# A six-layer decoder on one core: the routing of both expert mixtures rewritten, and the softmax behind the second routing moved down VectorE's queue

## The reference, cut to what matters

```python
def _L0_ffn_ref(hidden_states, Wr, W1, b1, Wo, bo, gamma, beta):
    router_logits = x @ Wr.T
    expert_idx = jnp.argmax(jax.nn.softmax(router_logits, axis=-1), axis=-1)
    for e in range(E):
        mask = (expert_idx == e)[:, None].astype(x.dtype)
        inter = inter + mask * jax.nn.gelu(x @ W1[e] + b1[e], approximate=False)
...
def _L1_ffn_ref(x, Wr, br, W1, b1, W2, b2):
    cap = max(1, int(T / E * CAPACITY_FACTOR))            # 40 slots of each of 8 experts
    probs = jax.nn.softmax(x @ Wr + br, axis=-1)
    topk_p, topk_e = jax.lax.top_k(probs, K)              # K = 2
    oh = jax.nn.one_hot(e_flat, E, dtype=jnp.int32)
    pos_all = jnp.cumsum(oh, axis=1) - oh                 # place of a token in its expert's slots
    keep = pos < cap
    h = jax.nn.relu(jnp.einsum('enc,ech->enh', buf, W1) + b1[:, None, :])
    y = jnp.einsum('enh,ehc->enc', h, W2) + b2[:, None, :]
    y_tok = y_tok * (p_flat * keep.astype(x.dtype))[:, :, None]
```

## Time and profile before

| | |
|---|---|
| median of 3 runs | 1101.97 us (1101.78 to 1103.04) |
| the profiled execution's own time | 1103.46 us |
| its span in the profile | 1101.5 us |
| PE busy | 1053.6 us, 96% of the span |
| DVE busy | 724.1 us, 66% |
| ACT busy | 643.1 us, 58% |
| POOL busy | 167.1 us, 15% |

### The profile page before, as it was taken

The page is one execution under the profiler, slowest core; times in us unless marked ns, Lnnn a source line. Parts: engine busy times, 40 slices in busy tenths (PEclk is TensorE's granted clock), DMA queues, the critical chain, the costliest instruction groups (busy, mean ns, idle before and its releaser), DMA issues.

```text
span 1101.5 us, 23000 instructions
## 1 busy us (share of the span) xinstructions
PE 1053.6 (96%) x9039; PEld 666.0 (60%) x9039; DVE 724.1 (66%) x1841; ACT 643.1 (58%) x1428; POOL 167.1 (15%) x237
## 2 busy tenths in 40 slices
PE   7999999998999999999899999999999999999987
PEld 5663665556875556555687366555578646655567
DVE  6641767889653386888955158688975417677871
ACT  5550557776763266777566136777666505587724
POOL 3320400121020130111112022021212004000000
PEclk9999999999999999999999999999999999999999
DMA  8400000000000000000000000000000000000000
GB/s 254 140 1 1 1 2 11 14 9 1 1 11 1 1 1 2 11 21 1 2 2 10 1 1 2 11 1 21 2 1 10 1 1 1 2 1 1 2 2 10
DMA packets 21083, 15.74 MB, mean 14 GB/s; under 512 B 887, under 2 KB 18660, under 8 KB 20972
## 3 DMA queue, kind: packets, MB, share of 16 engines
q1 hardware_dynamic: 20948, 14.24, 4.3%
q10 hardware_dynamic: 24, 0.01, 0.0%
HBM read 13.18 MB, written 1.05 MB: 13 GB/s over the span
## 4 chain that ended last, share of the span: by engine, by line
PE 72%; DVE 11%; ACT 9%; issue 5%; DVEq 2%; POOL 1%; POOLq 0%; ACTq 0%; DMA 0%
PE ps L786 11%; PE ps L1020 8%; PE ps L984 8%; PE ps L1002 5%; PE ps L828 3%; PE ps L822 3%; PE ps L1172 3%; PE ps L1163 3%; PE ps L1029 2%; ACT arena L1476 2%; PE ps L819 2%; PE ps L920 2%; DVE nmax L2186 2%; ACT arena L1239 2%; PE ps L880 2%
## 5 line engine op out<-in xcount | busy, mean ns | idle before, releaser
L1239 ACT ACTIVATE arena<-ps 128x512 f32<-128x512 f32 (+7 forms) x296 | 159.6, 572 | 111.3 <-PE ps L1002 55.6
L2186 DVE TENSOR_REDUCE nmax<-ps 128x1 f32<-128x512 f32 x256 | 164.4, 684 | 23.6 <-PE ps L984 22.9
L1476 ACT ACTIVATE arena<-ps,nmax 128x512 f32<-128x512 f32 x256 | 173.8, 685 | 7.9 <-DVE nmax L2186 4.8
L1652 POOL TENSOR_TENSOR rstd<-mv,neg_half 128x2 f32<-128x2 f32 x72 | 49.9, 695 | 660.6 <-DVE mv L1826 660.5
L1002 PEld LDWEIGHTS ps<-ident,arena 64*128 64x128 f32 x2048 | 76.5, 138 | 79.0 <-issue 45.4
L2191 DVE COPY arena<-ps 128x512 f32<-128x512 f32 x128 | 88.2, 689 | 47.5 <-PE ps L1002 47.2
L786 PE MATMUL ps<-big,w1a 128*128 128x512 f32 x256 | 117.3, 604 | 0.1
L1002 PE MATMUL ps<-ident,arena 64*128 64x64 f32 x2048 | 92.6, 228 | 8.1 <-ACT arena L1239 2.7
L2078 DVE TENSOR_TENSOR big<-XT,ps 128x512 f32<-128x512 f32 x32 | 22.0, 688 | 90.7 <-PE ps L771 90.4
L786 PEld LDWEIGHTS ps<-big,w1a 128*128 128x128 f32 x256 | 46.3, 189 | 57.7 <-issue 56.5
L1401 ACT ACTIVATE big<-ps 128x512 f32<-128x512 f32 x16 | 9.6, 597 | 116.4 <-PE ps L786 116.4
(11 more groups left out here) (393 smaller groups left out, 2009.1 us busy)
## 6 DMA issues: line engine op xcount, KB each, us to landing
ctx<-in_ctx_dram SPq DMA_DIRECT2D x4, 512.0 KB, 4.0
w1a<-in_L_ffn_W_dram SPq DMA_DIRECT2D x1, 2048.0 KB, 9.5
w1b<-in_L_ffn_W_dram SPq DMA_DIRECT2D x1, 2048.0 KB, 11.6
w2b<-in_L_ffn_W_dram SPq DMA_DIRECT2D x8, 256.0 KB, 6.0
X<-in_x_dram SPq DMA_DIRECT2D x4, 256.0 KB, 2.8
out_dram<-Y SPq DMA_DIRECT2D x3, 256.0 KB, 2.3
arena<-in_L_xattn_Wq_dram SPq DMA_DIRECT2D x1, 512.0 KB
arena<-in_L_xattn_Wk_dram SPq DMA_DIRECT2D x1, 512.0 KB
```

The costliest lines, as they stand in the source:

```text
L1239: return act.activation(dst, src, ACT.Copy)
L1476: act.activation(cprob[:, 2 * (t % 2) + h, :], bank(2 * (t % 2) + h), ACT.Exp, bias=nmax[:, s:s + 1], accum_out=rsum[:, j % 2, s:s + 1]).t ...
L2186: dve.tensor_reduce(nmax[:, s:s + 1], bank(s % 4), AX.X, ALU.max, negate=True)\
```

## The change

Three things change, in all four passes.

1. One-expert mixture: the four comparisons that make `onehot` become one instruction over all tiles. PE turns the one-hot before the keys (2, 0) instead of behind them, issues both picks one behind the other, and then the keys (3, 0), which go into bank 1 instead of bank 4. ACT copies `ohT` before the keys (2, 0).
2. Two-expert mixture, routing: the eight comparisons become two, the subtraction for the softmax goes behind the cast, the first half of the dispatch matrix is announced by itself (`disp_ready` counts two for each pass), and PE gathers the first sequence's tokens as soon as that half is there. The transposes that filled PE's time become fewer, and keys and values of the next pass are spread over the gaps. On ACT the exponentials come before the recurrence's sigmoid.
3. Two-expert mixture, softmax: sum, inverse and product of the exponentials go from between the cast and the places to the head of `combined()`, behind the recurrence's inverses, and a drain is added.

```diff
@@ PE, mixture_top1
                 project_v(0, 6, 1)
-                project_k(2, 7, 0)
                 keys_read(it, 0, 1)
                 pe.wait_ge(onehot_ready, it + 1)
...
                 last.then_inc(ohT_ps, 1)
+                project_k(2, 7, 0)
...
-                project_k(3, 4, 0)
                 pe.wait_ge(ohT_ready, it + 1)
                 pick_rows(0)
-                keys_read(it, 3, 0)
                 pick_rows(1)
+                project_k(3, 1, 0)
+                keys_read(it, 2, 0)
@@ PE, mixture_top2
                     turn_ctx(it + 1, 5)
-                    keep_awake(4, 4)
-                    for seq in range(GROUP):
-                        pe.wait_ge(ctxT_ready, (it + 1) * 2 + seq + 1)
-                        project_k(5, 3 + seq, seq)
+                    pe.wait_ge(ctxT_ready, (it + 1) * 2 + 1)
+                    project_k(5, 3, 0)
                 else:
-                    keep_awake(6, 32)
+                    keep_awake(6, 22)
...
-                    for seq in range(GROUP):
-                        project_v(5, seq, seq)
-                    keys_read(it + 1, 5, 1)
+                    pe.wait_ge(ctxT_ready, (it + 1) * 2 + 2)
+                    project_k(5, 4, 1)
+                    project_v(5, 0, 0)
                 else:
-                    keep_awake(6, 18)
-                pe.wait_ge(disp_ready, it + 1)
+                    keep_awake(6, 12)
                 for b in range(GROUP):
+                    if more:
+                        keys_read(it + 1, 5, b)
+                    pe.wait_ge(disp_ready, it * GROUP + b + 1)
...
+                if more:
+                    project_v(5, 1, 1)
                 pe.wait_ge(xb_ready, it * GROUP + GROUP)
...
-                    values_read(it + 1, 5, 1)
+                    values_read(it + 1, 5, 0)
                 up(0)
                 for e in range(E):
+                    if more and e == 0:
+                        values_read(it + 1, 5, 1)
@@ ACT, mixture_top2
                 if more:
-                    rec_receptance(it + 1, 7)
                     ctx_turned(it + 1, 5)
+                    keys(it + 1, 5, 3, 0)
                 act.wait_ge(e1_arg, it + 1)
                 act.activation(ex1[:, :, :], ex1[:, :, :], ACT.Exp).then_inc(e1_exp, 1)
                 if more:
-                    for seq in range(GROUP):
-                        keys(it + 1, 5, 3 + seq, seq)
-                    for seq in range(GROUP):
-                        context_values(it + 1, 5, seq, seq)
+                    rec_receptance(it + 1, 7)
+                    keys(it + 1, 5, 4, 1)
+                    context_values(it + 1, 5, 0, 0)
@@ DVE, mixture_top1
-                for t in range(TT):
-                    last = dve.tensor_scalar(onehot[:, t, :], iota_e[:, :], topf[:, t, 0:1], None, ALU.is_equal)
-                last.then_inc(onehot_ready, 1)
+                dve.tensor_tensor(onehot[:, :, :], iota_e[:, :].unsqueeze(1).to_broadcast([P, TT, PARTS * E]),
+                                  topf[:, :, 0:1].to_broadcast([P, TT, PARTS * E]), ALU.is_equal).then_inc(onehot_ready, 1)
@@ DVE, mixture_top2
-                for t in range(TT):
-                    dve.tensor_scalar(A[:, t, :], iota_e[:, 0:E], topf[:, t, 0:1], None, ALU.is_equal)
-                    dve.tensor_scalar(onehot[:, t, 0:E], iota_e[:, 0:E], topf[:, t, 1:2], None, ALU.is_equal)
+                for part, which in ((A[:, :, :], 0), (onehot[:, :, 0:E], 1)):
+                    dve.tensor_tensor(part, iota_e[:, 0:E].unsqueeze(1).to_broadcast([P, TT, E]),
+                                      topf[:, :, which:which + 1].to_broadcast([P, TT, E]), ALU.is_equal)
...
-                dve.wait_ge(e1_exp, it + 1)
-                dve.tensor_reduce(esum[:, :], ex1[:, :, :], AX.X, ALU.add)
...
+                for seq in range(GROUP):
+                    for t in tiles_of(seq):
+                        last = dve.tensor_tensor(slots(disp, t), iota_c[:, :].unsqueeze(1).to_broadcast([P, E, CAP]),
+                                                 per_expert(posA, t), ALU.is_equal)
+                    last.then_inc(disp_ready, 1)
                 dve.drain()
 
                 def combined():
+                    dve.wait_ge(e1_exp, it + 1)
+                    dve.tensor_reduce(esum[:, :], ex1[:, :, :], AX.X, ALU.add)
+                    dve.drain()
+                    dve.reciprocal(einv[:, :], esum[:, :])
```

More of the change, by code:

```diff
@@ L1540, in mixture_top2 @@
                     copy(xb[:, b, :], ps[:, 3 + b, 0:SLOTS]).then_inc(xb_ready, 1)
+                if more:
+                    context_values(it + 1, 5, 1, 1)
                 W = GROUP * CAP
@@ L2299, in mixture_top2 @@
                 dve.drain()
-                dve.tensor_tensor(ex1[:, :, :], lg[:, :, :], top[:, :, 0:1].to_broadcast([P, TT, E]), ALU.subtract)\
-                    .then_inc(e1_arg, 1)
                 for t in range(TT):
@@ L2313, in mixture_top2 @@
                 dve.tensor_copy(A_bf[:, :, :], A[:, :, :]).then_inc(two_hot, 1)
[L2315 to L2320 removed]
+                dve.tensor_tensor(ex1[:, :, :], lg[:, :, :], top[:, :, 0:1].to_broadcast([P, TT, E]), ALU.subtract)\
+                    .then_inc(e1_arg, 1)
                 dve.wait_ge(pos_ps, it + 1)
@@ L2331, in per_expert @@
                     return m[:, t, :].unsqueeze(2).to_broadcast([P, E, CAP])
-                for t in range(TT):
-                    last = dve.tensor_tensor(slots(disp, t), iota_c[:, :].unsqueeze(1).to_broadcast([P, E, CAP]),
-                                             per_expert(posA, t), ALU.is_equal)
-                last.then_inc(disp_ready, 1)
+                for seq in range(GROUP):
[3 more added lines that the diff above has]
+                    last.then_inc(disp_ready, 1)
                 dve.drain()
                 def combined():
+                    dve.wait_ge(e1_exp, it + 1)
+                    dve.tensor_reduce(esum[:, :], ex1[:, :, :], AX.X, ALU.add)
+                    dve.drain()
+                    dve.reciprocal(einv[:, :], esum[:, :])
+                    dve.drain()
+                    dve.tensor_tensor(ex1[:, :, :], ex1[:, :, :], einv[:, :].unsqueeze(2).to_broadcast([P, TT, E]),
+                                      ALU.mult)
+                    dve.drain()
                     for t in range(TT):
```

10 lines of the change are left out of this document (3 added, 7 removed).

## The result

The changed kernel takes 1094.87 us (median of 4 runs, 1094.07 to 1095.72); the kernel before took 1101.88 (4 runs, 1101.74 to 1103.04). The ratio is 0.993, with a 95% interval of 0.9915 to 0.9945. The prediction was 1094.9.

The account below looks back on a forecast made before the run. The prediction took PE's pace as the bound (72% of the last chain), with DVE's queue nearly tied. Its terms, 4 × 0.5 + 2.85 + 2.25 = 7.1 us, took the median from 1101.97 to 1094.9, own range 1093.9 to 1096.6.

Parts of the forecast that it names:

- One-expert mixture: predicted 0.5 in each pass: One-expert mixture, four times: one wide comparison and PE's new order start the first expert 0.5 us earlier, bounds 0.2 to 0.6.
- Two-expert mixture, passes 1 to 3: predicted 0.95 each: Passes 1 to 3: DVE's shorter routing starts the recurrence's second norm 0.95 us earlier in each, 2.85 in all.
- the second rival: Eight routings: longer counting wait, 0.43 comparisons and DVE stalls lose 0.3 to 0.45 us each, giving 1097.3 to 1098.5; chance 0.17.
- the new wait of 0.3 to 0.5 that I named as a sign: Passes 1 to 3: PE newly waits 0.3 to 0.5 us for DVE ahead of the second norm's turn.
- Last pass: predicted 2.25: Pass 4, without a recurrence: only routing counts, and the first expert starts 2.25 us earlier.
- PE's side in full: Passes 1 to 3: the combine chain costs DVE nothing new, each gains 1.4 us, total 8.5, 1093.5; chance 0.10.
- The table load: ACT: a load costs 2.66 us with its drain, bank 4 is freed late, gain 6.4, 1095.6; chance 0.03.
- That the comparisons are no shorter: Both mixtures' routing: wide comparisons take as long as those they replace, gain 1.5 us, 1100.5; chance 0.07.
- The clock: PE around the routings: less filler lowers TensorE's clock, 9.3 us lost make the kernel 0.2% slower; chance 0.03.

Follow-up runs that it names:

- The run with forty memsets: Changed kernel with forty tiny memsets and forty drains added at the head of DVE's list: 1100.82 us, ratio 0.9985.
- The run with one part alone: Kernel before with only the one-expert mixture's part of the change: 1099.65 us, ratio 0.9971.
- the kernel without the chain: Changed kernel with the two-expert softmax's sum, inverse and product left out, so part of the computation is missing: 1092.29 us, ratio 0.9903.
- with the sigmoid first: Changed kernel with the recurrence's sigmoid again ahead of the context's copies and the exponentials on ACT: 1095.95 us, ratio 0.9936.
- with it on POOL: Changed kernel with the softmax's sum, inverse and product moved from DVE to POOL: 1092.59 us, ratio 0.9909.
- with it ahead: Changed kernel with sum, inverse and product of the exponentials again between the cast and the places on DVE: 1097.82 us, ratio 0.9955.
- the two-expert part alone: Changed kernel with the one-expert mixture put back as before: 1096.79 us, ratio 0.9946.

## Why the prediction was right, and where its sizes were off

**The bound.** PE's pace sets the time, and only its gaps around the routings could be won. The experiments agree: what an edit gained or lost in the interval behind a routing stands in net, up to the pauses, and the loads saved on ACT moved it by 0.2 at most.

**One-expert mixture: predicted 0.5 in each pass, measured 0.32 to 0.34** (0.60 in pass 4, where a pause of before is gone). The comparison was right, 0.26. Three spacings on PE were 0.1 too short, and that is why the term is too large. The turns start at 2.08 behind the logits and not 1.99, since PE starts 0.14 behind the one-hot's end (73.27 to 73.41) instead of the 0.06 that I took from the counting, a product of another kind (128x8 in bf16, not 128x128 in f32). Keys are followed by a pick after 0.95 (73.85 to 74.80) and by the expert's product after 0.97 (75.33 to 76.30), not 0.86; I had taken the spacing of like instructions. The first expert so comes at 4.97 instead of 4.69, only 0.22 earlier than before; another 0.1 comes back in the expert's first product, 3.60 instead of 3.70. The term is 1.59 where I had 2.0, inside the bound of 0.2 to 0.6 for each.

**Two-expert mixture, passes 1 to 3: predicted 0.95 each, measured 0.63, 0.99, 0.98.** The steps hold one by one in passes 2 and 3: places at 2.89 (predicted 2.90), the wait for the counting with the subtraction ahead of it as long as I took it, the gather at 4.55 (4.58), the norm 0.97 earlier (0.95). Pass 1 lost the pause of 0.43 ahead of its cast, which is the mechanism of the second rival, with its price, in one routing of eight. The run with forty memsets shows it: without that pause pass 1 is like the other two. Only the split was off. PE gained 1.65 up to the first expert and not 1.4, and is held by DVE for 0.7 and not 0.45, in two places and not one; the new wait of 0.3 to 0.5 that I named as a sign shows up as 0.17 and 0.21. Both errors are the same size, so the sum came out.

**Last pass: predicted 2.25, measured 2.25.** The run with one part alone shows that 0.34 of it is a pause of before and not the change. I had counted that pause into the old length without saying so.

**What the sum left out.** By my terms the change is worth 6.44 instead of 7.1. Against that stand 1.22 us of pauses that DVE no longer makes between the mixtures, and the two make 7.66, not 7.0. The rest is the start. Going over to the median was right for before, where three of four runs have the early start (1101.74 to 1101.97), but of the four runs of after two are early (1094.07, 1094.26) and two late (1095.47, 1095.72), and the median 1094.87 lies between. Early runs against early runs differ by 7.7. So the median hit to 0.03 us is luck: 0.66 too much in the terms, 1.22 that no term had, and 0.65 lost again by which starts the runs happened to have.

**The rivals.** PE's side in full does not hold: the kernel without the chain is the one that shows it, 2.2 us further on by its intervals. The table load costs 1.28 and no more. The Trainium skill, ScalarE: Activation LUTs, section "What ACT_TABLE_LOAD costs", adds a drain of 1.38; here the load starts 0.02 behind the exponentials' end and the next activation at 274.87, 0.01 behind the load's end at 274.86. That the comparisons are no shorter is refuted by the kernel that goes back to them: 5.1 us slower by its intervals, 6.6 with pauses. The Trainium skill, VectorE: DVE Perf Modes, section "Mode 2×_2P", speaks for the old form by its rate; here eight comparisons of 8 elements took 1.43 us from first to last (274.50 to 275.93, with a gap of 0.16 among them), and two of 32 take 0.30 (272.03 to 272.33). The formula of the same page of the Trainium skill, with 151 fixed cycles, gives as an estimate 0.19 for 32 elements, and the trace shows 0.19. The clock did not fall in the routings of after, where it is 1.00; without the filler that was kept in pass 4 it falls there.

## What to carry to other kernels

Tiny operations in a routing cost nearly the same whatever their size, so join them first; reordering the waiting engine's list paid here mostly once the results came sooner. When work is moved off one critical queue, look for an engine that stands idle rather than for a later place on the same queue: 3.6 times slower on POOL was still 2 us better. And compare traces by intervals inside the kernel, since the start and the pauses move whole microseconds that belong to no edit; look at TensorE's granted clock in the first microseconds before two medians are compared.

## What the runs showed of the hardware

- DVE's pauses of about 0.42 us belong to places in its instruction list. Six kernels whose DVE lists agree up to there (the changed one, those without filler, with the sigmoid first, without the chain, with it on POOL, with it ahead) pause at the same cast in pass 1, though their starts differ by 1.5 us. With 16 entries more at the head of the list the pause stands 16 entries earlier. With the two-expert part alone, whose one-expert routing has three comparisons more, it stands three entries earlier, at the drain ahead of the sum (0.32 of it shows). The row of the kernel without filler:

```profile
274.49 0.18 DVE L2311 CAST A_bf<-A 128x32 bf16<-128x32 f32 x1 [0.43 <-issue]
```

  And that of the two-expert part alone:

```profile
273.62 0.19 DVE L2314 TENSOR_TENSOR A<-A,onehot 128x32 f32<-128x32 f32 x1 [0.32 <-issue]
```

  Net differed by up to 1.1 us between kernels that compute the same in the same order. What the engine does in a pause stays open; fetching of instructions would fit, and no run here separates it from other causes.
- Executions fall into two groups some 1.6 us apart, and the difference lies ahead of the first router (71.1 to 71.6 or 72.8 to 73.0). It goes with TensorE's granted clock from 8 to 12 us, 1.00 or 0.57 to 0.63. In the slow stretch two products of 128x256 (hT with kv_more) take 1.06 instead of 0.59. In the late traces PE had waited longer for the DMA of the column rows before (0.94 to 1.47, against 0.25 to 0.78). No run moved that wait by itself, so that it is the cause is argued and not shown.
- Around two waits of PE of 2.59 and 1.25 us (the filler of pass 4 left out) the granted clock was 0.50 from within the first until 1067.00, and 1.00 again from 1068.00 on.
- A tiny memset with a drain took 0.16 on DVE in a row of forty (28 in 4.56).
- A power of -1 on 128x4 took 1.07 on POOL; additions of 16, 8 and 4 elements took 0.22 to 0.42 there.
